# Two neighbouring attentions of a decoder kernel in one block, interleaved by batch slots

## The chip, the cores and the metric

The kernel runs on one core of one Trainium2 chip, in one launch. The metric is device microseconds of the whole launch, the median of several runs; lower is better.

## The reference, cut to what matters

The model is a decoder of four layers with three sublayers each (attention, cross attention, feed forward). Each sublayer takes the rows `x` (16 batches of 128 tokens, width 256), normalises them, and adds its result to `x`. The change is in the first two sublayers:

```python
def _L0_attn_ref(x, Wq, Wk, Wv, Wp, bp):          # "l0a", 16 heads of 16, one chunk of 128 tokens
    phi_q = elu(heads(x @ Wq.T)) + 1.0
    phi_k = elu(heads(x @ Wk.T)) + 1.0
    A = where(tril, einsum('bhncd,bhnsd->bhncs', phi_q, phi_k), 0.0)
    num, den = einsum('bhncs,bhnse->bhnce', A, vh), A.sum(-1) + EPS
    return merge(num / den[..., None]) @ Wp.T + bp

def _L0_xattn_ref(q, k, v, attention_mask, ...):  # "l0x": q from x, k and v from the context
    scores = einsum('bnlh,bnph->bnlp', qm, km) / sqrt(16)
    scores = where(mask, scores, -1e8)
    return merge(einsum('bnlp,bnph->bnlh', softmax(scores), vm)) @ Wo.T + bo
```

Both read the layer norm of `x`: each batch is normalised by the mean and the variance of its own rows, so batch b of l0x needs only batch b of l0a's result.

## The kernel before, in words

All rows stay in one tile `x` on the chip (128 partitions, 256 columns for each of the 16 batches), with a mean and a variance for each batch in `mean_var` (`G.mv`). The program is a chain of stages, listed in `STAGES`. Each stage opens a block in which every engine gets its own instruction list, written out in order; semaphores tie the lists together. At its end `Region.close` (line 82) ends the block, clears the stage's semaphores and puts a barrier over all engines (line 89), so that nothing of a stage runs beside the one before.

Stage l0a is `transposed_attention` (line 263), stage l0x is `softmax_attention` (line 625). Both are software pipelines over the 16 batches, and the engines' lists are loops over a step i. In l0a TensorE does at step i: `scores(i)` (L407), `weigh_values(i-1)` (L427), `transpose_x(i+2)` (L373), `project_out(i-2)` (L436), `project_qk(i+2)` (L389) and `project_v(i+2)` (L395). ScalarE copies the second half of the scores (L500), takes the denominators (L509), the transposed rows (L471) and the exponentials of q and k (L484), and normalises rows for later (L464). VectorE forms the features (L564), masks half of the scores (L576), divides (L580, L583), adds the result to x (L590) and takes its statistics three steps behind (L594, L598). GpSimd spreads the heads (L339), masks the other half (L348) and adds the output bias (L353).

In l0x TensorE does at step i: `scores(i)` (mask L769, products L778), the four `transpose_p(i-1)` (L789) with `weigh_values(i-2)` (L806), `transpose_x(i+2)` (L731) and the projections of batch i+2 (L747, L753, L759) between them, and `project_out(i-2)` (L813). The scores of a batch fill all four banks of `psS`, so `scores(i)` waits for the exponentials of batch i-1. VectorE takes maxima (L1002) and ScalarE the exponentials with their sums (L883), VectorE inverts the sums (L1009), GpSimd scales (L706). Before its loop l0x prepares on VectorE: two normalised batches (L933), the mask as float (L965) and as filling values (L976).

The layer norm needs a square root on ScalarE and an inverse on VectorE. l0a takes them for the first 12 batches in its own tail (`early_roots` L159, `early_inverse` L165); l0x takes the last four at its start (L170, L176). ScalarE loads another function table when it goes from exponentials to roots or back.

PSUM has eight banks. Each of the two stages uses all eight: four for the scores and one each for four other uses.

Of the kernel before, what the change touches and what calls it, by code (L numbers as in the profile page):

```python
# [17 lines left out]
P = 128  # L18
NB = 16
# [133 lines left out]
HEAD = 12  # L153

# [108 lines left out]
def transposed_attention(nc, G, A, tag, kind, w, cross=False, out_bias=False):  # L263
# [6 lines left out]
    if G.next == "l0x":  # L270
        load_early(nc, G, "l0x", attention_loads(nc, G, A, "l0x"))
        loads = loads + G.ahead
# [22 lines left out]
    psS, psXV, psQK, psO, psY = R.ps("psS", [P, 2048]), R.ps("psXV", [P, 512]), R.ps("psQK", [P, 512]), R.ps("psO", [P, 512]), R.ps("psY", [P, 512])  # L295
# [9 lines left out]
    block = R.block()  # L305
# [7 lines left out]
    @block.sync  # L313
    def _(sp):
        for dst, src, sem in loads:
            sp.dma_start(dst, src).then_inc(sem, 16)
        sp.wait_ge(loaded, NL)
        sp.wait_ge(G.context_loaded, 16)

    @block.gpsimd  # L320
    def _(pool):
# [7 lines left out]
        nc.gpsimd.memset(G.pad[:, 0:1], 0.0).then_inc(set_up, 1)  # L329
        pool.wait_ge(loaded, NL)  # L330
# [33 lines left out]
    @block.tensor  # L364
    def _(pe):
# [74 lines left out]
        for i in range(-2, NB + 2):  # L440
            if 0 <= i < NB:
                scores(i)
# [10 lines left out]
    @block.scalar  # L453
    def _(act):
# [59 lines left out]
        for i in range(-2, NB + 1):  # L514
            if not relu2 and 0 <= i < NB:
# [14 lines left out]
        early_roots(nc, G, act, mv_ready, head_ready)  # L530

    @block.vector
    def _(dve):
# [66 lines left out]
        for i in range(-3, NB + 3):  # L600
            if not relu2 and 0 <= i + 1 < NB:
# [13 lines left out]
            if i == NB + 1:  # L615
# [3 lines left out]
        dve.wait_ge(inverse_ready, 1)  # L619
        dve.wait_ge(mv_ready, NB)  # L620

    close_stage(G, R)


def softmax_attention(nc, G, A, tag, kind, w, normed="layer", cross=False, biased=False, out_bias=False, saved=None, ahead=()):
# [12 lines left out]
    st6 = R.sb("st6", [P, 6 * NB])  # L638
    mask2 = R.sb("mask2", [P, 2])
# [7 lines left out]
    rstd, std = G.rstd, G.std  # L647
# [13 lines left out]
    psS, psT, psXV, psQK, psOY = R.ps("psS", [P, 2048]), R.ps("psT", [P, 512]), R.ps("psXV", [P, 512]), R.ps("psQK", [P, 512]), R.ps("psOY", [P, 512])  # L661
# [3845 lines left out]
```

## Time and profile before

| | |
|---|---|
| median of 3 runs | 2493.9 us (2491.03 to 2498.77) |
| profiled execution, span from first to last instruction | 2493.0 us (the profile gives its span alone) |
| TensorE busy over the span | 2221.8 us, 89% |
| VectorE, ScalarE, GpSimd busy | 1680.9, 1318.5, 805.3 us |
| mean granted TensorE clock | 0.944 of full speed |
| stage l0a | from 13.0 to 139.5 us |
| stage l0x | from 140.7 to 310.4 us |

Busy shares are averages over stages with different limits. A timeline line gives a start, a duration, the engine and source line, what is written from what, and in brackets the idle time of the engine before it with what ended it. Where several equal instructions follow each other they stand as one line with a count, and the duration is that of all together.

### The profile page before, as it was taken

What the parts mean: (1) busy time and instruction counts of PE and PEld (TensorE: products, weight loads), DVE (VectorE), ACT (ScalarE), POOL (GpSimd) and SP (SyncE); (2) the same over time, 40 slices, a digit from 0 to 9 for tenths busy, and PEclk for the clock granted to TensorE, in tenths of its full rate; (3) what the DMA queues carried; (4) which work ended last, traced back from release to release, by engine and by line L of the source; (5) the groups of instructions that cost most, each with busy time, mean ns of one, the idle gap of its engine ahead of it and who ended that gap; (6) DMA issues with size and microseconds to landing.
All of it is one profiled execution on the core that took longest, in us unless ns stands there. A gap on an engine that the chain in (4) does not pass through costs nothing. (4 is left out here: it accounts for less than half of the span.)

```text
span 2493.0 us, 48623 instructions
## 1 busy us (share of the span) xinstructions
PE 2221.8 (89%) x17358; PEld 1814.4 (73%) x17360; DVE 1680.9 (67%) x3260; ACT 1318.5 (53%) x3083; POOL 805.3 (32%) x1019
## 2 busy tenths in 40 slices
PE   6979799999699797989999979999779897999875
PEld 5857587887476696778888658888567686788652
DVE  4767544774666586765677646666677785888858
ACT  4558635665477663542666443333476574445335
POOL 4656402333255442100233202222211100544365
PEclk9989879999899898979999999999889999999888
DMA  3000082113400000032211430000200002877711
GB/s 113 2 1 2 1 338 83 52 52 131 147 2 2 22 2 1 2 157 115 100 52 51 163 130 1 2 1 1 102 1 1 1 1 88 229 207 214 230 29 34
DMA packets 102933, 178.37 MB, mean 72 GB/s; under 512 B 59687, under 2 KB 71591, under 8 KB 97578
## 3 DMA queue, kind: packets, MB, share of 16 engines
q1 hardware_dynamic: 85514, 135.93, 16.4%
q0 software_dynamic: 9792, 28.85, 3.6%
q10 hardware_dynamic: 7392, 10.49, 1.2%
q8 instruction: 144, 2.36, 0.4%
q14 instruction: 91, 0.75, 0.1%
HBM read 112.44 MB, written 62.78 MB: 70 GB/s over the span
## 5 line engine op out<-in xcount | busy, mean ns | idle before, releaser
L2356 POOL TENSOR_TENSOR l2a_Pn<-l2a_Pn,l2a_rden 128x1024 f32<-128x1024 f32 x32 | 60.0, 1897 | 288.9 <-DVE l2a_rden L2595 288.9
L1630 ACT ACTIVATE l0f_w_parts<-l0f_W 128x512 fp32r (+1 forms) x117 | 90.4, 775 | 64.8 <-PE l0f_psG L1435 50.4
L1788 DVE TENSOR_TENSOR l0f_w_parts<-l0f_W,l0f_w_parts 128x512 fp32r<-128x512 f32 (+1 forms) x117 | 99.2, 867 | 37.7 <-ACT l0f_w_parts L1630 37.5
L1630 ACT ACTIVATE l1f_w_parts<-l1f_W 128x512 fp32r (+1 forms) x117 | 90.5, 774 | 63.1 <-PE l1f_psG L1435 50.3
L4188 POOL TENSOR_TENSOR l3x_Pn<-l3x_Pn,l3x_fac 128x616 f32<-128x616 f32 (+2 forms) x96 | 70.3, 761 | 150.3 <-DVE l3x_fac L4267 140.6
L1788 DVE TENSOR_TENSOR l1f_w_parts<-l1f_W,l1f_w_parts 128x512 fp32r<-128x512 f32 (+1 forms) x117 | 99.2, 867 | 12.6 <-ACT l1f_w_parts L1630 12.2
L1488 PE MATMUL l1f_psY<-l1f_W,l1f_XT_hT 128*128 (+1 forms) x440 | 104.2, 380 | 0.8 <-ACT l1f_XT_hT L1610 0.8
L883 ACT ACTIVATE l1a_att_Pn<-l1a_att_psS,l1a_att_nmx 128x128 f32<-128x128 f32 x256 | 91.8, 418 | 1.7 <-DVE l1a_att_nmx L1002 1.7
L883 ACT ACTIVATE l0x_Pn<-l0x_psS,l0x_nmx 128x128 f32<-128x128 f32 x256 | 91.7, 418 | 0.9 <-DVE l0x_nmx L1002 0.9
L706 POOL TENSOR_TENSOR l1a_att_Pn<-l1a_att_Pn,l1a_att_rden 128x512 f32<-128x512 f32 x64 | 66.5, 1039 | 72.1 <-DVE l1a_att_rden L1009 72.1
L1488 PEld LDWEIGHTS l1f_psY<-l1f_W,l1f_XT_hT 128*128 128x128 f32 x440 | 80.3, 190 | 10.8 <-issue 1.0
L706 POOL TENSOR_TENSOR l0x_Pn<-l0x_Pn,l0x_rden 128x512 f32<-128x512 f32 x64 | 66.5, 1039 | 51.3 <-DVE l0x_rden L1009 49.3
L1765 DVE TENSOR_TENSOR l1f_work<-l1f_work,l1f_psU 128x512 f32<-128x512 f32 x55 | 37.8, 687 | 64.3 <-PE l1f_psU L1435 41.7
L1368 POOL DMA_INDIRECT results_by_token<-l0f_rows_in_out,l0f_dest x39 | 38.8, 995 | 130.0 <-DVE l0f_rows_in_out L1776 130.0
L1368 POOL DMA_INDIRECT results_by_token<-l1f_rows_in_out,l1f_dest x39 | 38.5, 987 | 130.6 <-DVE l1f_rows_in_out L1776 130.6
L4259 DVE TENSOR_TENSOR_SCAN l3x_cum<-l3x_segments_begin,l3x_Pn 128x1024 f32<-128x1024 f32 x32 | 73.4, 2292 | 8.3 <-ACT l3x_Pn L4119 8.3
L1488 PE MATMUL l0f_psY<-l0f_W,l0f_XT_hT 128*128 x312 | 73.9, 380 | 0.8 <-ACT l0f_XT_hT L1610 0.8
L1359 POOL DMA_INDIRECT l1f_rows_in_out<-rows_by_token,l1f_source x39 | 37.9, 972 | 101.2 <-DVE pad L1853 74.0
L883 ACT ACTIVATION_READ_ACCUMULATOR l0x_Pn<-l0x_psS,l0x_nmx 128x1 f32 x256 | 66.4, 259 | 0.0
L883 ACT ACTIVATION_READ_ACCUMULATOR l1a_att_Pn<-l1a_att_psS,l1a_att_nmx 128x1 f32 x256 | 66.3, 259 | 0.0
L2516 ACT ACTIVATE l2a_Pn<-l2a_Pn 128x1024 f32<-128x1024 f32 x32 | 33.9, 1058 | 59.9 <-DVE l2a_Pn L2587 59.9
L1359 POOL DMA_INDIRECT l0f_rows_in_out<-rows_by_token,l0f_source x39 | 38.1, 977 | 84.8 <-DMA keys<-l0f_rows_in_out 67.5
(883 smaller groups left out, 7652.5 us busy)
## 6 DMA issues: line engine op xcount, KB each, us to landing
relative_rows<-l3x_ext SPq DMA_DIRECT2D x32, 516.0 KB, 5.9
l1f_W<-in_l1f_w SPq DMA_DIRECT2D x9, 1536.0 KB, 20.1
l0f_W<-in_l0f_w SPq DMA_DIRECT2D x8, 1536.0 KB, 26.4
cumulative_rows<-l3x_cum SPq DMA_DIRECT2D x32, 384.0 KB, 3.4
l3x_K<-keys SPq DMA_DIRECT2D x16, 512.0 KB, 5.2
l3x_rel<-relative_rows SPq DMA_DIRECT2D x32, 231.0 KB
values<-l1f_W SPq DMA_DIRECT2D x11, 512.0 KB, 5.6
l3x_V<-values SPq DMA_DIRECT2D x16, 308.0 KB
```

Source lines behind the costliest of these rows:

```text
L706: nc.gpsimd.tensor_tensor(part, part, rden[b % 2][:, 4 * r:4 * r + 4].unsqueeze(2).to_broadcast([P, 4, P]), ALU.mult)\
L883: ins = nc.scalar.activation(Pn[b % 2][:, pos * P:(pos + 1) * P], psS[:, pos * P:(pos + 1) * P], ACT.Exp, bias=nmx[b % 2][:, pos:pos + 1], ...
L1359: nc.gpsimd.indirect_dma_start(X[k % NX][:, :], None, G.XN[:, :], bass.IndirectOffsetOnAxis(source[:, k:k + 1], 0))\
L1368: nc.gpsimd.indirect_dma_start(G.YT[:, :], bass.IndirectOffsetOnAxis(dest[:, k:k + 1], 0), Y[k % NY][:, :], None)\
L1488: ins = nc.tensor.matmul(psY[:, 0:D], hT[n % 2][:, j * P:(j + 1) * P], weights(n, 2 * DC * F + j * D, D), start=(j == 0), stop=(j == FC - 1))
L1630: nc.scalar.activation(w_high[i], W[:, bass.ds(act_offsets[k] + o, m)], ACT.Copy).then_inc(high_ready, 1)
L1765: nc.vector.tensor_tensor(h[n % 2], sg[n % 2], psU[:, :], ALU.mult).then_inc(h_ready, 1)
L1788: nc.vector.tensor_tensor(w_low[i], W[:, bass.ds(dve_offsets[k] + o, m)], w_high[i], ALU.subtract).then_inc(low_ready, 1)
L2356: nc.gpsimd.tensor_tensor(part, part, rden[b % 2][:, 8 * u:8 * u + 8].unsqueeze(2).to_broadcast([P, 8, P]), ALU.mult)\
L2516: nc.scalar.activation(part, part, ACT.Exp, scale=W ** -0.5).then_inc(e_ready, 1)
L4188: nc.gpsimd.tensor_tensor(v, v, fac[n % 3][:, s * HH:(s + 1) * HH].unsqueeze(2).to_broadcast([P, HH, SEG[s]]), ALU.mult)\
L4259: nc.vector.tensor_tensor_scan(cum[i][:, :], segments_begin[:, :], Pn[n % NP][:, :], 0.0, ALU.mult, ALU.add).then_inc(sums_ready, 1)
```

## The change: both stages in one block

The two functions no longer open a block: each returns a `Part` with one generator for each engine, which yields a slot number ahead of each step's instructions. `run_parts` opens one block, and `by_slots` writes each engine's list by drawing from the generators in order of slot, the first attention first at equal slots. The second attention's slots lie 16 (its predecessor's number of batches) behind: its step i is slot 16+i. So on each engine the second's fill (steps -2 and -1) comes in slots 14 and 15, behind the first's own steps there, and its first scores in slot 16. What comes ahead of the first yield (GpSimd's clearing of five value tiles, VectorE's head scales) is written at the start of the block. VectorE prepares the mask in slots 6, 8 and 10. The layer norm's roots for the second attention are taken in two parts: batches 0 to 7 in slot 12 (ScalarE) and 13 (VectorE, with the first two normalised batches), batches 8 to 15 in slots 19 and 20. The first attention's `early_roots` and `early_inverse` go. The PSUM banks are allocated once and used by both; where the second first writes a bank, TensorE waits for the last read of it by the first. The end and the start of a block between the two go, with semaphore clearing and barrier. The first attention of layer 1 and the cross attention of layer 1 use the same functions, each as the single part of its block.

```diff
+FIRST = 8
+
+def by_slots(*programs):
+    todo = [[next(program) + offset, k, program, offset] for k, (program, offset) in enumerate(programs)]
+    while todo:
+        now = min(todo, key=lambda entry: entry[:2])
+        slot = next(now[2], None)
+        if slot is None:
+            todo.remove(now)
+        else:
+            now[0] = slot + now[3]
+
+def run_parts(nc, G, *parts):
+    offsets = [0]
+    for part in parts[:-1]:
+        offsets.append(offsets[-1] + part.slots)
+    K = Region(nc, "parts")
+    block = K.block()
...
+    @block.tensor
+    def _(pe):
+        by_slots(*[(part.tensor(pe), o) for part, o in zip(parts, offsets)])
...
+def attention_banks(R):
+    return {name: R.ps(name, [P, size]) for name, size in (("psS", 2048), ("psXV", 512), ("psQK", 512), ("psM", 512), ("psN", 512))}
...
 def transposed_attention
+    def projections_read(eng):
+        eng.wait_ge(xnT_ready, NB)
+        eng.wait_ge(v_ready, NB)
+    def queries_read(eng):
+        eng.wait_ge(qk_ready if relu2 else qk_taken, NB)
+    def scores_read(eng):
+        eng.wait_ge(pa_raw if relu2 else pa_ready, NB)
+        eng.wait_ge(pb_raw, NB)
+    def sums_read(eng):
+        eng.wait_ge(oT_ready, NB)
+        eng.wait_ge(den_ready, NB)
+    def rows_read(eng):
+        eng.wait_ge(x_ready, NB)
...
         for i in range(-2, NB + 1):
+            yield i
...
-        early_roots(nc, G, act, mv_ready, head_ready)
+        if last:
+            early_roots(nc, G, act, mv_ready, head_ready)
...
 def softmax_attention: tensor
             if b >= 1:
                 pe.wait_ge(v_ready, b)
+            elif before:
+                before.projections_read(pe)
...
         def scores(b):
+            if b == 0 and before:
+                before.scores_read(pe)
...
 scalar
-        if layer:
+        if before:
+            yield -4
+            act.wait_ge(before.moments_ready, FIRST)
+            nc.scalar.activation(std[:, 0:FIRST], variances(G)[:, 0:FIRST], ACT.Sqrt, bias=G.neg1e5[:, 0:1]).then_inc(first_roots, 1)
+        elif layer:
             late_roots(nc, G, std_ready)
...
             new, now, mid = i + 2 < NB, 0 <= i < NB, 0 <= i - 1 < NB
+            yield i
+            if before and i == 3:
+                act.wait_ge(before.moments_ready, NB)
+                nc.scalar.activation(std[:, FIRST:], variances(G)[:, FIRST:], ACT.Sqrt, bias=G.neg1e5[:, 0:1]).then_inc(std_ready, 1)
...
 vector
-        normalise(0)
-        normalise(1)
-        if layer:
-            late_inverse(nc, G, dve, step, std_ready)
+        if before:
             head_scales()
+            yield -10
+        else:
+            normalise(0)
+            normalise(1)
+            if layer:
+                late_inverse(nc, G, dve, step, std_ready)
+                head_scales()
...
             step.do(nc.vector.memset(ones[:, :], 1.0))
+            yield -8
...
+            yield -6
             step.do(nc.vector.tensor_scalar(fill[:, :], mbc[:, :], -1.0, piece[:, 0:1], ALU.add, ALU.mult))
...
+            yield i
+            if before and i == -3:
+                dve.wait_ge(first_roots, 1)
+                nc.vector.reciprocal(rstd[:, 0:FIRST], std[:, 0:FIRST]).then_inc(first_inverse, 1)
+                dve.wait_ge(first_inverse, 1)
+                dve.wait_ge(before.moments_ready, FIRST)
+                normalise(0)
+                normalise(1)
+            if before and i == 4:
+                dve.wait_ge(before.moments_ready, NB)
+                dve.wait_ge(std_ready, 1)
+                step.do(nc.vector.reciprocal(rstd[:, FIRST:], std[:, FIRST:]))
...
+def first_attentions(nc, G, A):
+    C = Region(nc, "l0")
+    banks = attention_banks(C)
+    G.held.append(C)
+    load_early(nc, G, "l0x", attention_loads(nc, G, A, "l0x"))
+    parts = [transposed_attention(nc, G, A, "l0a", "linear", "l0a_", out_bias=True, banks=banks, last=False)]
+    parts.append(softmax_attention(nc, G, A, "l0x", "masked", "l0x_", cross=True, biased=True, out_bias=True, banks=banks, before=parts[0]))
+    run_parts(nc, G, *parts)
...
-    "l0a": lambda nc, G, A: transposed_attention(nc, G, A, "l0a", "linear", "l0a_", out_bias=True),
-    "l0x": lambda nc, G, A: softmax_attention(nc, G, A, "l0x", "masked", "l0x_", cross=True, biased=True, out_bias=True),
+    "l0a": first_attentions,
+    "l0x": lambda nc, G, A: None,
```

## Rows read from the trace of the kernel before

**Rows 1.** Stages: us, busy by engine (count), PEclk, DMA share, GB/s.

```profile
13.00:140.70 127.70, 114.26 (x1696) 94.72 (x1696) 78.36 (x117) 62.73 (x117) 70.00 (x73) 0.98 0.07 26
...
140.70:311.60 170.90, 145.99 (x1504) 112.94 (x1504) 115.97 (x300) 123.04 (x596) 99.64 (x117) 0.93 0.01 2
```

**Rows 2.** Timeline, end of the first attention: start us, us, engine, line, op.

```profile
131.13 0.30 PE L427 MATMUL l0a_psO<-l0a_PTa,l0a_V 128*32 128x128 f32 x2 [1.86 <-DVE l0a_oT L583]
...
136.11 0.17 DVE L598 BATCH_NORM_AGGREGATE mean_var<-l0a_st 128x2 f32<-128x6 f32 x1
...
136.22 0.43 DVE L594 BATCH_NORM_STATS2 l0a_st<-x 128x6 f32<-128x256 f32 x1
...
139.36 0.18 DVE L598 BATCH_NORM_AGGREGATE mean_var<-l0a_st 128x2 f32<-128x6 f32 x1
```

**Rows 3.** Timeline, start of the second attention.

```profile
140.73 1.74 POOL L688 MEMSET l0x_V<- 128x512 f32 x3 [11.05 <-POOLq L89]
...
140.77 1.24 DVE L933 TENSOR_SCALAR l0x_xn<-x,mean_var,rstd 128x256 f32<-128x256 f32 x2 [1.23 <-PEq L89]
...
142.52 1.51 DVE L965 CAST l0x_mbc<-l0x_w_m 128x2048 f32<-128x2048 uint8 x1
...
145.07 1.29 DVE L976 TENSOR_SCALAR l0x_fill<-l0x_mbc,l0x_piece 128x2048 bf16<-128x2048 f32 x1
...
148.14 0.41 PE L731 MATMUL l0x_psXV<-ident,l0x_xn 128*128 128x128 f32 x2 [0.69 <-DVE l0x_V L996]
...
151.88 0.40 PE L769 MATMUL l0x_psS<-l0x_fill,l0x_ones 32*128 32x512 bf16 x4
```

**Rows 4.** Timeline, TensorE at batches 14 and 15 of the first attention.

```profile
120.30 1.15 PE L407 MATMUL l0a_psS<-l0a_bd,l0a_qk 32*128 32x256 f32 x16
...
121.37 0.30 PE L427 MATMUL l0a_psO<-l0a_PTa,l0a_V 128*32 128x128 f32 x2
...
124.32 1.15 PE L407 MATMUL l0a_psS<-l0a_bd,l0a_qk 32*128 32x256 f32 x16
```

**Rows 5.** Timeline, first softmax batch up to the second's scores.

```profile
153.21 1.29 DVE L1002 TENSOR_REDUCE l0x_nmx<-l0x_psS 128x4 f32<-128x512 f32 x2 [0.29 <-PE l0x_psS L778]
...
155.77 1.19 PE L747 MATMUL l0x_psQK<-l0x_xnT,l0x_w_Wq 128*128 128x128 f32 x8 [2.26 <-ACT l0x_xnT L863]
...
156.76 1.90 PE L753 MATMUL l0x_psQK<-ctxT,l0x_w_Wk 128*128 128x128 f32 x8
...
158.46 1.88 PE L759 MATMUL l0x_psXV<-l0x_w_Wv,ctxT 128*128 128x256 f32 x4
...
160.28 0.39 PE L769 MATMUL l0x_psS<-l0x_fill,l0x_ones 32*128 32x512 bf16 x4
```

**Rows 6.** Timeline, ScalarE and VectorE waits in a first-attention batch.

```profile
114.66 1.02 ACT L500 ACTIVATE l0a_PTb<-l0a_psS 128x1024 f32<-128x1024 f32 x1 [0.61 <-PE l0a_psS L407]
...
119.54 0.60 ACT L484 ACTIVATE l0a_ex<-l0a_psQK 128x512 f32<-128x512 f32 x1 [2.24 <-PE l0a_psQK L389]
...
120.65 0.69 DVE L564 SCALAR_TENSOR_TENSOR l0a_qk<-l0a_ex,l0a_re 128x512 f32<-128x512 f32 x1 [0.97 <-ACT l0a_re L485]
```

**Rows 7.** Timeline, ScalarE: table loads and root at the boundary.

```profile
133.64 1.28 ACT L159 ACT_TABLE_LOAD   x1
...
134.93 0.30 ACT L159 ACTIVATE std<-mean_var,ln_eps 128x12 f32<-128x12 f32 x1
...
151.76 1.28 ACT L883 ACT_TABLE_LOAD   x1
```

**Rows 8.** Timeline, ScalarE between two softmax batches.

```profile
177.72 0.74 ACT L872 ACTIVATE l0x_qk<-l0x_psQK,l0x_w_bq 128x128 f32<-128x128 f32 x2
...
180.01 0.60 ACT L891 ACTIVATE l0x_PT<-l0x_psT 128x512 f32<-128x512 f32 x1 [1.55 <-PE l0x_psT L789]
...
180.50 0.36 ACT L883 ACTIVATE l0x_Pn<-l0x_psS,l0x_nmx 128x128 f32<-128x128 f32 x1
```

**Rows 9.** A stretch of low granted clock, columns of Rows 1.

```profile
156.00:160.00 4.00, 4.00 (x20) 3.47 (x19) 1.80 (x5) 4.00 (x25) 2.84 (x3) 0.60 0.00 0
```

More of the change, by code:

```diff
@@ L304, in transposed_attention @@
     s_step, p_step = R.sem("dve_step"), R.sem("pool_step")
-    block = R.block()
+    part = Part(R, loads, loaded, NL)
+    part.slots, part.moments_ready = NB, mv_ready
+    def projections_read(eng):
[11 more added lines that the diff above has]
+        eng.wait_ge(x_ready, NB)
+    part.projections_read, part.queries_read, part.scores_read, part.sums_read, part.rows_read = projections_read, queries_read, scores_read, sums_read, rows_read
     NV = 4
@@ L311, in heads, with gpsimd @@
         return 4 * r + 2 * c
[L313 to L321, printed above, removed]
+    def gpsimd(pool):
         step = Step(pool, p_step)
@@ L362, in _, with tensor @@
                 add_bias(i)
-    @block.tensor
-    def _(pe):
+    def tensor(pe):
+        yield -2
         pe.wait_ge(loaded, NL)
@@ L614, in _ @@
                 add_y(i - 2)
-            if i == NB + 1:
+            if last and i == NB + 1:
                 early_inverse(nc, G, dve, head_ready, inverse_ready)
@@ L618, in _, with softmax_attention @@
                 moments(i - 3)
-        dve.wait_ge(inverse_ready, 1)
+        if last:
+            dve.wait_ge(inverse_ready, 1)
         dve.wait_ge(mv_ready, NB)
-    close_stage(G, R)
-def softmax_attention(nc, G, A, tag, kind, w, normed="layer", cross=False, biased=False, out_bias=False, saved=None, ahead=()):
+    part.gpsimd, part.tensor, part.scalar, part.vector = gpsimd, tensor, scalar, vector
+    return part
+def softmax_attention(nc, G, A, tag, kind, w, normed="layer", cross=False, biased=False, out_bias=False, saved=None, ahead=(), banks=None, before=None):
     masked = kind == "masked"
@@ L670, in softmax_attention @@
     s_step, p_step = R.sem("dve_step"), R.sem("pool_step")
-    block = R.block()
+    part = Part(R, loads, loaded, NL)
+    part.slots, part.moments_ready = NB, mv_ready
     scale = HD ** -0.5
@@ L676, in heads, with gpsimd @@
         return 4 * r + 2 * c
-    @block.sync
-    def _(sp):
-        for dst, src, sem in loads:
-            sp.dma_start(dst, src).then_inc(sem, 16)
-        sp.wait_ge(loaded, NL)
-    @block.gpsimd
-    def _(pool):
+    def gpsimd(pool):
         step = Step(pool, p_step)
@@ L721, in _, with tensor @@
                 add_bias(i)
-    @block.tensor
-    def _(pe):
+    def tensor(pe):
+        yield -2
         pe.wait_ge(loaded, NL)
@@ L800, in weigh_values @@
                 pe.wait_ge(x_ready, b)
+            elif before:
+                before.rows_read(pe)
             for c in range(DC):
```

74 lines of the change are left out of this document (56 added, 18 removed).

## The prediction

> **What bounds the kernel now.** I read the page first: its busy shares are averages over the whole program, and the chain of waits covers only the last 80 us, so neither says what this change is worth. The stage table does [rows 1]. While the first attention runs, TensorE is busy for 114 of 128 us at nearly full clock; in the second for 146 of 171 us, with ScalarE at 123. The reader is to see that TensorE's idle time in the first stage is 13.4 us and that it lies at the two ends. The timeline of the boundary shows where [rows 2]: the last batch is weighed at 131.13, after TensorE waited 1.86 us for the division, and the stage's last moment is finished at 139.54. Then barrier and fill [rows 3]: GpSimd starts at 140.73, VectorE makes the mask (1.51 us, then 1.29 us), the second batch's fill starts on TensorE at 148.14, and the first softmax scores only at 151.88.
>
> **The time between two marks.** One mark is the start of scores of batch 14 in the first attention, at 120.30 [rows 4]; the other the start of the second scores of the softmax attention, at 160.28 [rows 5]. Before it is 39.98 us. I build the same stretch from the new lists of TensorE.
>
> Slot 14: scores, weighing and output projection as now, 124.32 - 120.30 = 4.02 us [rows 4]. Behind them the fill of softmax batch 0. Its price is the fill of batch 1 at full clock, 151.88 - 148.14 = 3.74 us [rows 3]. Together 7.76. What the fill waits for on the banks (last rows, values and projections of batch 15 copied) is done in slot 13, so I take that wait as nothing; at worst it is the copy and its handshake, 0.6 us. Slot 15 is the same: 7.76. In slot 16 weighing and projection come first, 124.32 - 121.37 = 2.95 us [rows 4]. So the softmax scores start at 120.30 + 18.47 = 138.77, against 151.88: 13.11 us earlier. This takes with it the barrier, the mask, the late normalising and the division waits, since TensorE has other work during each.
>
> **Maxima come late in slot 16.** VectorE finishes the first attention's step ahead of them. Batch 15 is weighed from 135.82 on; from there to the end of add and moment it is 136.28 - 131.13 = 5.15 us [rows 2], so the first maxima start at 140.97. By the old distance from scores to maxima, 153.21 - 151.88 = 1.33 us [rows 3, 5], they would start at 140.10. Loss: 0.87 us. From maxima to the second scores nothing changes, as TensorE waits for the exponentials there: 8.40 us from scores to scores, so the second mark would be at 138.77 + 0.87 + 8.40 = 148.04.
>
> **What is left of the first attention in slots 17 and 18.** Statistics 0.43 and moment 0.17 us [rows 2], and an add, taken as long as the statistics, stand ahead of the maxima of slot 17, and 0.60 of the same ahead of those of slot 18. All on the path would be 1.63 us, all hidden 0. ScalarE takes a transposed block before it needs the maxima (0.5 us, from 180.01 to 180.50 [rows 8]), which hides about that much each time: 0.6 and 0.2, so 0.8 us.
>
> **Preparations moved into the first attention.** In a steady step VectorE idles 0.97 us before the features [rows 6]. In slot 6 the mask conversion (1.51 [rows 3]) and two smaller instructions, for which I take 0.5, push the features by about 1.0; in slot 10 the filling values (1.29) by 0.3; the three small ones of slot 8 fit in. Behind the features stand the masking of scores, and on GpSimd the spreading; TensorE needs both a step later, so TensorE's order hides it: 0, at most 1.1 us for each. GpSimd's clearing of five tiles (three take 1.74 us [rows 3]) stands at the block's start, where it has nothing to spread yet. The roots in slot 12: load 1.28 and root 0.30 [rows 7] follow the copy of values, where ScalarE idles 0.61 us [rows 6], so the copy of scores comes 0.95 late; the masking by GpSimd behind it is needed a step later. Exponentials come back in slot 13, where ScalarE idles 2.24 us [rows 6]: hidden. VectorE's inverse (some 0.2) and two normalised batches (1.24 [rows 3]) in slot 13 stand against the 0.97 idle, 0.5 late, hidden likewise. Sum 0; with the cover gone it is the 0.95 plus 0.5. SyncE issues the same loads in the same order, and its waits hold nothing else.
>
> **The second half of the roots, slot 19.** This sits in the softmax loop, where ScalarE is on the path. Now: q taken until 178.46, the transposed block from 180.01, exponentials from 180.50 [rows 8]. After: a load of 1.28 and the root of 0.30 fill the idle 1.55; the block goes at 180.04; a load of 1.28 before the exponentials puts them at 181.92: 1.42 us late, and every batch after it. Bounds: 0 if TensorE has slack there, 2.86 if nothing is covered. At the old boundary both loads were beside waits.
>
> The trace puts no gap around a load: the one at 151.76 has no idle time before it, and the root at 134.93 starts with the load's end [rows 7].
> The Trainium skill, "ScalarE: Activation LUTs", section "What ACT_TABLE_LOAD costs", adds a drain of about 1.38 us to each load of 1.28. By that the slot would cost 2.76 us more; the trace does not agree so far.
>
> **The clock.** When TensorE had idled 2.26 us before the projections at 155.77, the engine's granted clock fell, to a mean of 0.60 from 156 to 160 [rows 5, 9], the upper level of 2.4 GHz and the lower of 1.2 mixed, and the projections took 1.70 and 1.82 instead of 0.99 (k and v against q). It was hidden then. In the new slot 16 the idle is 3.1 us (2.26 + 0.87), so I expect the same fall. Projections start at 138.77 + 0.87 + 3.89 (155.77 - 151.88) = 143.53; q 0.99, k 1.70, v 1.88, and behind them, newly, the first attention's last output projection, as long as v: 1.88. They end at 149.98, 1.94 us behind the mark of 148.04. At full clock they end near 147.4 and cost nothing. I take 1.94; bounds 0 and 3.0 (all four at the low level).
>
> **Sum.** 13.11 - 0.87 - 0.80 - 0 - 1.42 - 1.94 = 8.08 us. The profiled span is 2493.0; after it 2484.9. The median of the runs is 0.9 above the span, which I take as what lies around it: 2493.9 - 8.1 = 2485.8. Later stages move earlier as a whole; no transfer was started by the clock of a stage before them (GB/s is 2 in the second stage [rows 1]).
>
> **Rivals.**
> - The clock holds in slot 16: 10.0 us gained, 2483.9. For it, work is denser before the idle time than in the old slot; against it, the idle is longer.
> - Each switch of tables holds ScalarE longer in the loop than the 1.28 shown. If as much again per switch (2.56), the gain is 5.5: 2488.4. For it: the loop is the one place where exponentials stand right on both sides; against it rows 7. The Trainium skill's section named above states such an addition.
> - The overlap doesn't do what it says: VectorE, in order, waits for the fill's values and keys of slot 14 and 15 before masking the first attention's scores, and TensorE waits for those; fill and drain alternate. Then only what lies between 139.54 and the start of a fill 3.74 us before 148.14 goes, 4.9 us, of which 1.42 and 0.80 are paid back: 2.7 us, 2491.2. Against it: the values come 1 us before the scores TensorE issues next.
> - Slower: the clock falls in slot 16 or at the switch in slot 19 and stays low. A batch holds 146 / 16 = 9.1 us of TensorE work at 0.93 [rows 1] in a period of about 9 (8.40 for the first [rows 3, 5]), so at the lower level (k took 1.70 against 0.99) it takes some 15.5 us, 6.5 lost. From two such batches on the gain of 10.0 is gone; 13 lost is 2497. Against it: the fall within 156 to 160 [rows 9] was over by the scores at 160.28, whose four mask products took 0.39 us as those at 151.88 took 0.40 [rows 3, 5].
>
> **How the numbers follow.** Chances: forecast 0.42, clock holds 0.26, longer switch 0.13, alternating 0.11, slower 0.08. What a measurement can tell from no change is 0.3%, 7.5 us: faster means under 2486.4. The forecast lies 0.6 us beyond it, and the runs of before spread over 7.7 us, so I give its case 0.6 faster, the clock case 0.85, the switch 0.2, and the others none beyond noise: 0.25 + 0.22 + 0.03 and a little, 0.52 faster. Slower by over 7.5 us needs three low batches: 0.07. The rest, 0.41, is within. The range: below, the clock case with slots 17 to 19 half hidden (another 1.1) and the spread of a median, 2480.5; above, the alternating case with some of that spread, 2492.0.
>
> **What would show it.** In the profile after: softmax scores near 138.8 and second scores near 149 to 150; no idle time on TensorE over 1 us from 120 to 139 but for the transposes; loads in slots 12, 13 and two in slot 19, with the distance between score starts there 1.4 longer than beside it; first maxima behind the moment of batch 13. Wrong would be: TensorE waiting in slots 14 or 15 for VectorE, steps of slots 6 to 13 longer than before, or a low granted clock beyond slot 17.

## The result and the profile after

In the first comparison the changed kernel took 2485.28 us (median of 8 runs, 2481.32 to 2489.73) against 2493.72 (8 runs, 2487.62 to 2498.77): ratio 0.9967, 95% interval 0.9954 to 0.998, which is 5.0 to 11.5 us faster. The forecast was 2485.8. A later comparison on another chip gave 2481.52 (5 runs, 2478.22 to 2482.98) against 2492.31 (11 runs): 0.9949, interval 0.9936 to 0.9961. The profiled execution spans 2483.9 us, 9.1 less than before.

The stage windows of the changed kernel, cut where the first softmax scores start and where the last ends; the columns are those of [rows 1]:

```profile
13.00:138.80 125.80, 118.68 (x1737) 99.38 (x1738) 81.54 (x128) 65.92 (x124) 74.48 (x82) 1.00 0.07 25
138.80:300.90 162.10, 137.07 (x1465) 105.90 (x1464) 111.90 (x290) 122.57 (x591) 93.57 (x109) 0.96 0.01 2
```

The first attention's stretch now holds 41 more matmul records (the two fills) in 1.9 us less, and TensorE idles 7.1 us in it instead of 13.4 [rows 1]. Its mean granted clock is 1.00 instead of 0.98.

TensorE's timeline of the changed kernel shows the two fills and the first slot with both attentions. To be compared with [rows 3 to 5]:

```profile
120.59 1.15 PE L484 MATMUL l_psS<-l0a_bd,l0a_qk 32*128 32x256 f32 x16
...
125.37 1.16 PE L834 MATMUL l_psQK<-l0x_xnT,l0x_w_Wq 128*128 128x128 f32 x8 [0.47 <-ACT l0x_xnT L961]
...
128.22 1.15 PE L484 MATMUL l_psS<-l0a_bd,l0a_qk 32*128 32x256 f32 x16
...
138.80 0.39 PE L858 MATMUL l_psS<-l0x_fill,l0x_ones 32*128 32x512 bf16 x4
...
143.45 1.69 PE L834 MATMUL l_psQK<-l0x_xnT,l0x_w_Wq 128*128 128x128 f32 x8 [3.02 <-ACT l0x_xnT L961]
144.93 1.92 PE L840 MATMUL l_psQK<-ctxT,l0x_w_Wk 128*128 128x128 f32 x8
146.64 1.37 PE L846 MATMUL l_psXV<-l0x_w_Wv,ctxT 128*128 128x256 f32 x4
147.84 1.03 PE L513 MATMUL l_psN<-l0a_w_Wo,l0a_oT 128*128 128x256 f32 x4
148.80 0.39 PE L858 MATMUL l_psS<-l0x_fill,l0x_ones 32*128 32x512 bf16 x4
```

Slots 14 and 15 take 7.63 us each (128.22 - 120.59), the fill standing behind the first attention's own step without any wait but the 0.47 for the transposed rows. The softmax scores start at 138.80 and the second ones at 148.80. In between TensorE idles 3.02 us, and of the four groups of products behind the idle time the first ones are slow: q takes 1.69 us instead of 1.16, k 1.92 instead of 1.06, the values 1.37 instead of 1.03. The projection at 147.84 is at full speed again (1.03).

What became of each interval, from score starts of both timelines. Only the starts of scores are in the table; slots are those of the changed kernel:

| stretch | before | after | saved |
|---|---|---|---|
| scores of batch 14 to first softmax scores | 120.30 to 151.88 = 31.58 | 120.59 to 138.80 = 18.21 | 13.37 |
| slot 16 | 8.40 | 10.00 | -1.60 |
| slots 17 and 18 | 17.85 | 17.97 | -0.12 |
| slot 19 (two table loads) | 8.99 | 10.42 | -1.43 |
| slot 20 | 9.00 | 9.12 | -0.12 |
| slot 21 to the last softmax scores | 90.96 | 90.96 | 0 |
| sum | | | 10.10 |

So the change is worth 10.1 us up to the last softmax scores (277.27 against 287.08, and 0.29 that the changed kernel was late at its batch 14, where the table begins). From the last softmax scores to TensorE's first product in stage l0f it is 24.30 us against 25.22, another 0.9 gained. From there to its first product in l3f this execution took 1.7 us more than the one before (2104.44 against 2102.73). Experiments 3 and 10 show that two executions of one program can differ by more than that, so it can't be put down to the change. With these pieces the 9.1 us between the spans are accounted for to 0.1.

VectorE in slot 16, and at the start of slot 17:

```profile
138.38 1.75 DVE L659 RECIPROCAL l0a_rden<-l0a_den 128x256 f32<-128x256 f32 x1 [1.15 <-ACT l0a_den L587]
...
140.83 0.17 DVE L677 BATCH_NORM_AGGREGATE mean_var<-l0a_st 128x2 f32<-128x6 f32 x1
140.93 1.25 DVE L1109 TENSOR_REDUCE l0x_nmx<-l_psS 128x4 f32<-128x512 f32 x2
...
149.62 0.17 DVE L677 BATCH_NORM_AGGREGATE mean_var<-l0a_st 128x2 f32<-128x6 f32 x1
150.13 1.29 DVE L1109 TENSOR_REDUCE l0x_nmx<-l_psS 128x4 f32<-128x512 f32 x2 [0.35 <-PE l_psS L867]
```

The maxima of slot 16 start right behind the first attention's moment, 2.13 us behind the scores instead of 1.33: 0.80 late. In slot 17 the leftovers are over before the scores are there: VectorE waits 0.35 us for TensorE.

ScalarE with its table loads, in slot 12 and in slot 19:

```profile
114.36 1.28 ACT L945 ACT_TABLE_LOAD   x1
115.66 0.30 ACT L945 ACTIVATE l0x_std<-mean_var,ln_eps 128x8 f32<-128x8 f32 x1
115.86 1.01 ACT L578 ACTIVATE l0a_PTb<-l_psS 128x1024 f32<-128x1024 f32 x1
...
167.13 1.28 ACT L996 ACT_TABLE_LOAD   x1
168.43 0.30 ACT L996 ACTIVATE l0x_std<-mean_var,ln_eps 128x8 f32<-128x8 f32 x1
168.66 0.60 ACT L989 ACTIVATE l0x_PT<-l_psM 128x512 f32<-128x512 f32 x1
169.27 1.28 ACT L981 ACT_TABLE_LOAD   x1
170.56 0.37 ACT L981 ACTIVATE l0x_Pn<-l_psS,l0x_nmx 128x128 f32<-128x128 f32 x1
```

Loads and their neighbours follow each other within 0.02 us. That is the place of the forecast's 1.42 us.

Two windows of the changed kernel show the low granted clock in slot 16, and the full one in slot 19 behind 1.96 us of idle time, with TensorE's queries there:

```profile
144.00:148.00 4.00, 4.00 (x19) 3.83 (x18) 1.57 (x4) 4.00 (x23) 2.53 (x3) 0.59 0.00 0
172.00:176.00 4.00, 3.59 (x26) 3.17 (x27) 3.16 (x9) 4.00 (x22) 2.37 (x3) 1.00 0.00 0
```

```profile
172.40 1.16 PE L834 MATMUL l_psQK<-l0x_xnT,l0x_w_Wq 128*128 128x128 f32 x8 [1.96 <-ACT l0x_xnT L961]
```

### The profile page after: what moved, and what is told of

The parts are those of the page before. It is cut to its first block and busy times, and to the rows that moved or that the text cites. A ratio compares the mean times of both kernels' runs of the same rounds, so it can differ in the third digit from the quotient of the medians.

```text
span 2483.9 us, 48616 instructions
## 1 busy us (share of the span) xinstructions
PE 2216.7 (89%) x17358; PEld 1810.0 (73%) x17360; DVE 1678.0 (68%) x3260; ACT 1322.2 (53%) x3085; POOL 803.3 (32%) x1019
## 3 DMA queue, kind: packets, MB, share of 16 engines
q8 instruction: 144, 2.36, 0.4%
## 5 line engine op out<-in xcount | busy, mean ns | idle before, releaser
L981 ACT ACTIVATE l0x_Pn<-l_psS,l0x_nmx 128x128 f32<-128x128 f32 x256 | 91.7, 417 | 3.3 <-DVE l0x_nmx L1109 3.3
L1608 PEld LDWEIGHTS l1f_psY<-l1f_W,l1f_XT_hT 128*128 128x128 f32 x440 | 80.3, 190 | 10.8 <-issue 1.0
L981 ACT ACTIVATION_READ_ACCUMULATOR l0x_Pn<-l_psS,l0x_nmx 128x1 f32 x256 | 66.1, 258 | 0.0
```

The costliest lines, as they stand in the source:

```text
L981: ins = nc.scalar.activation(Pn[b % 2][:, pos * P:(pos + 1) * P], psS[:, pos * P:(pos + 1) * P], ACT.Exp, bias=nmx[b % 2][:, pos:pos + 1], ...
L1608: ins = nc.tensor.matmul(psY[:, 0:D], hT[n % 2][:, j * P:(j + 1) * P], weights(n, 2 * DC * F + j * D, D), start=(j == 0), stop=(j == FC - 1))
```

## The experiments

Kernels 1 to 8 were each executed once with a profile, beside one execution of the kernel before on the same chip (2496.45 or 2496.2 us). A total from one execution says little, as the runs of one kernel spread over 5 to 11 us, so their verdicts rest on distances within the first 280 us, taken from the scores of batch 14. These distances repeat: in a second profile of the changed kernel on another chip (kernel 9) the one to the last softmax scores is 156.88 us instead of 156.68.

### 1. The second attention three slots later

Its fill and first scores then have none of the first attention's work beside them; the block, the prepared mask and the two-part roots stay.

```diff
-        offsets.append(offsets[-1] + part.slots)
+        offsets.append(offsets[-1] + part.slots + 3)
...
```

The lines left out move the yields of roots and mask by as many slots the other way, so these stay where they were.

> One block as in the changed kernel, but the second attention's steps lie 19 slots behind instead of 16, with its mask and first roots left in slots 6 to 12. TensorE then fills only behind the first attention's last projection. Theory: barrier and preparations are one part of what was gained, the fill beside the drain's waits the larger one. Drain as in the kernel before, to about 138.4 us, then two fills of 3.7 to 6.6 us by the clock: first softmax scores at 146 to 149 instead of 138.8, span 2484 + 8 = 2492 or so. Rival: what was gained is the block's end and the preparations, and the interleaving is worth little: first scores within 2 us of 138.8 and span at 2484 to 2486.

Measured: 2498.12 us beside 2496.45. TensorE around the first softmax scores, and in the slot with the table loads:

```profile
148.07 0.39 PE L858 MATMUL l_psS<-l0x_fill,l0x_ones 32*128 32x512 bf16 x4
...
180.04 2.08 PE L834 MATMUL l_psQK<-l0x_xnT,l0x_w_Wq 128*128 128x128 f32 x8 [1.97 <-ACT l0x_xnT L961]
```

The batch-14 scores of this execution are 1.10 us later than before's, so the softmax scores come 4.9 us earlier than before (151.88 - 148.07 + 1.10). That is what the missing barrier and the moved preparations bring by themselves. The other 8.5 of the 13.4 us comes with the interleaving. It includes what the clock gives: from 136 to 144 us the granted clock is 0.88 and 0.70 here, where the change has 1.00 and 0.99. Without the interleaving next to nothing remains: the slot with the table loads costs 11.82 us here instead of 8.99, and at the last softmax scores 1.5 us of the 4.9 is left (121.40 to 286.66 is 165.26 us, before it is 166.78). About half of what that slot loses is the table swap (1.43 in the change); the other 1.4 is a fall of the clock, 0.58 from 180 to 184 us, which the change does not have there.

### 2. One slot earlier

```diff
-        offsets.append(offsets[-1] + part.slots)
+        offsets.append(offsets[-1] + part.slots + -1)
...
```

Here too the lines left out keep roots and mask in their slots.

> The second attention's steps lie 15 slots behind instead of 16, its mask and first roots stay in slots 6 to 12. Theory: TensorE's only long idle stretch left (3.0 us at 140.4) comes from exponentials that start late, so an earlier first softmax batch fills it with the first attention's last weighing and projection: first scores near 136.8, second near 146 instead of 148.8, span 2 to 3 us less, 2481 to 2482. Rival: PSUM handover and in-order VectorE bring new waits (scores of batch 0 behind the last masked scores, transposes behind the last division), which eat it: second scores at 148 or later, span 2484 or more.

Measured: 2486.88 us. TensorE:

```profile
137.33 0.39 PE L858 MATMUL l_psS<-l0x_fill,l0x_ones 32*128 32x512 bf16 x4
...
141.98 2.08 PE L834 MATMUL l_psQK<-l0x_xnT,l0x_w_Wq 128*128 128x128 f32 x8 [3.03 <-ACT l0x_xnT L961]
...
149.28 0.39 PE L858 MATMUL l_psS<-l0x_fill,l0x_ones 32*128 32x512 bf16 x4
```

Taken from the scores of batch 13 (114.35 here, 113.74 in the change), the first softmax scores come 2.08 us earlier, the second 0.13 earlier and the last 1.05 later: the first attention's last batch now stands, with weighing and division, inside the first softmax batch, and TensorE runs out of work there just the same. The forecast of 2 to 3 us less was wrong: the second scores are not earlier by more than 0.13 us, as the rival had it. Sixteen slots is the best distance of the three.

### 3 and 10. The mask prepared late

VectorE's cast and filling values in slot 13, against the first attention's work, instead of slots 6, 8 and 10.

```diff
-            yield -10
+            yield -3
...
-            yield -8
+            yield -3
...
-            yield -6
+            yield -3
```

> Undoes one part: VectorE prepares the whole mask (some 3.9 us) in slot 13, ahead of the roots' inverse and the first two normalised batches, instead of in slots 6, 8 and 10. Theory: in slots 6 to 10 it costs nothing because TensorE needs VectorE's results a step later, while 3.9 us at once run past that slack of about 2 to 3 us: the scores of batch 15 or the weighing of batch 14 start 1 to 2 us late, span 2485 to 2486. Rival A: hidden here too, second scores at 148.8 within 0.2. Rival B: no slack at all, 3.9 us late, span 2488.

Measured: 2479.13 us. VectorE, with the features behind all of it:

```profile
120.07 1.19 DVE L1070 CAST l0x_mbc<-l0x_w_m 128x2048 f32<-128x2048 uint8 x1
...
122.29 1.29 DVE L1083 TENSOR_SCALAR l0x_fill<-l0x_mbc,l0x_piece 128x2048 bf16<-128x2048 f32 x1
...
124.51 0.68 DVE L643 SCALAR_TENSOR_TENSOR l0a_qk<-l0a_ex,l0a_re 128x512 f32<-128x512 f32 x1
```

The features come at 124.51 instead of about 121, and TensorE's next scores still start 7.63 us behind the last ones (120.76 to 128.39); to the last softmax scores it is 156.77 us against 156.68. Even this heavier load in one slot is hidden, where 1 to 2 us of delay had been expected (rival A was right). The 6.5 us that the total lies below the change's are made where the edit touches nothing: from TensorE's first product in l0f to its first in l3f this execution took 2097.50 us, the change's 2104.44. So I ran the same kernel again, timed:

> The mask preparations moved to slot 13 once more, now timed in five rounds. Its one profiled execution was 6.5 us below the change's, all of it in stages that the edit doesn't touch. Theory (that was the later stages' wander): median within 2 us of the change's on this chip, about 2485. Rival (each program keeps its own time in the later stages, because its code lies otherwise or its stages start at another phase of the clock): it stays 4 us or more below the change, and the later stages' marks agree with those of the single execution to under 1 us.

Measured: 2484.04 us (6 runs, 2478.9 to 2485.68), 2.5 above the change on the same chip (within 2 had been expected), with widely overlapping runs. Its profiled execution took 2105.87 us from l0f to l3f: the same program, on another chip, 8.4 us apart in the same stages. On the one chip its six runs already spread over 6.8 us. That excludes the rival that each program keeps its own time in the later stages: the later stages wander from execution to execution, and no difference of a few us in them may be put down to an edit of the first attentions.

### 4. The root from the logarithm

The inverse root as exp(-0.5 ln(v)), for one table if both functions shared it with the exponentials.

```diff
-            nc.scalar.activation(std[:, 0:FIRST], variances(G)[:, 0:FIRST], ACT.Sqrt, bias=G.neg1e5[:, 0:1]).then_inc(first_roots, 1)
+            nc.scalar.activation(std[:, 0:FIRST], variances(G)[:, 0:FIRST], ACT.Ln, bias=G.neg1e5[:, 0:1]).then_inc(first_roots, 1)
+            act.wait_ge(first_roots, 1)
+            nc.scalar.activation(rstd[:, 0:FIRST], std[:, 0:FIRST], ACT.Exp, scale=-0.5).then_inc(first_inverse, 1)
...
```

The second eight roots are edited in the same way, and VectorE's two inverses go.

> The second attention's inverse roots are taken on ScalarE as exp(-0.5 ln(v + eps)), two functions that one table can hold, instead of root and inverse; everything else is as in the changed kernel. Theory: the 10.42 us between the softmax scores of batches 3 and 4, against 8.99 beside them, is the two table loads of slot 19 less 1.4 us of idle time: the distance becomes 8.99 to 9.1 and everything behind moves 1.4 us, and the 0.13 us of the inverse in slot 20 goes too; span 2482.4. Rival: the 1.43 us is the wait for the first attention's last moments in slot 19, or the compiler loads a table for each of the two functions: the distance stays at 10.4 or grows.

Measured: 2486.72 us. ScalarE:

```profile
114.55 1.28 ACT L945 ACT_TABLE_LOAD   x1
...
116.16 1.28 ACT L947 ACT_TABLE_LOAD   x1
...
170.08 1.28 ACT L998 ACT_TABLE_LOAD   x1
...
171.69 1.28 ACT L1000 ACT_TABLE_LOAD   x1
```

A load stands ahead of the logarithm and another ahead of the exponential behind it, so nothing is saved, as the rival had it: slot 19 takes 10.53 us. It shows the price of bad cover, however. The two loads in slot 12, with only the logarithm between them, lengthen the stretch from the scores of batch 13 to those of batch 14 from 6.85 to 8.20 us, where one load in slot 12 and one in slot 13 had cost nothing.

Slot 16, which the edit does not touch, takes 11.32 us here instead of 10.00:

```profile
144.99 2.08 PE L834 MATMUL l_psQK<-l0x_xnT,l0x_w_Wq 128*128 128x128 f32 x8 [3.04 <-ACT l0x_xnT L963]
```

Behind the same idle time as in the change (3.04 against 3.02 us) k and the values take 1.91 us each and the first attention's projection 1.45; the granted clock is 0.53 from 144 to 148 and 0.61 from 148 to 152, where the change has 0.59 and 1.00. So the same idle time ahead of the same products can cost 1.3 us more in one kernel than in another.

### 5. Roots without ScalarE

A guess from the bits of the variance and three Newton steps on VectorE, spread over slots 11, 12, 19 and 20; no table load is left there.

```diff
-                nc.scalar.activation(std[:, FIRST:], variances(G)[:, FIRST:], ACT.Sqrt, bias=G.neg1e5[:, 0:1]).then_inc(std_ready, 1)
...
+                step.do(nc.vector.tensor_scalar(y.bitcast(U32), v.bitcast(U32), -0.5, 1597463007.0, ALU.mult, ALU.add))
...
+                step.do(nc.vector.tensor_tensor(t, y, y, ALU.mult))
+                step.do(nc.vector.scalar_tensor_tensor(t, t, -0.5, v, ALU.mult, ALU.mult))
+                step.do(nc.vector.scalar_tensor_tensor(y, t, 1.5, y, ALU.add, ALU.mult))
...
```

> The second attention's inverse roots are worked out on VectorE alone, from a guess by the bits of the number and three Newton steps (eleven small instructions for each half), in pieces put ahead of places where VectorE waits anyway; ScalarE has no root and no table load between slots 12 and the end. Theory: the distance between the softmax scores of batches 3 and 4 falls from 10.42 to 9.0 us, that of 4 and 5 from 9.12 to 9.0, everything behind is 1.4 to 1.6 us earlier than in the changed kernel from one mark to the other. Rival: the small instructions are too long for VectorE's waits, the maxima of the next banks go late and half or more of the 1.4 us comes back.

Measured: 2480.99 us. Slot 19 takes 9.09 us instead of 10.42, slot 20 takes 9.65 instead of 9.12. VectorE in slot 20 shows why:

```profile
176.82 1.25 DVE L1122 TENSOR_REDUCE l0x_nmx<-l_psS 128x4 f32<-128x512 f32 x2
177.99 0.35 DVE L1021 TENSOR_TENSOR l0x_tmp<-l0x_rstd 128x8 f32<-128x8 f32 x1
178.38 0.54 DVE L1022 SCALAR_TENSOR_TENSOR l0x_tmp<-l0x_tmp,l0x_std 128x8 f32<-128x8 f32 x1
178.95 0.54 DVE L1023 SCALAR_TENSOR_TENSOR l0x_rstd<-l0x_tmp,l0x_rstd 128x8 f32<-128x8 f32 x1
179.52 0.69 DVE L1135 COPY l0x_PT<-l_psM 128x512 f32<-128x512 f32 x1
```

The three small operations stand ahead of the copy that TensorE's weighing waits for. Two of them take 0.54 us each. The same three on the same columns take 0.16, 0.17 and 0.17 us in slot 19 (from 170.48 on). GpSimd is at work from 176.58 to 179.46 and idle from 170.35 to 171.33, and each of these small operations in this trace that falls into idle time of GpSimd takes 0.13 to 0.17 us. That points at GpSimd's work beside them as what makes them long; no run sets it apart. The table swap did cost what slot 19 showed: 1.33 of it comes back, and 0.53 is paid in slot 20.

### 6, 7 and 8. The idle time ahead of the second batch's queries

Three ways to deal with TensorE's 3.02 us. Kernel 6 moves the first attention's last output projection into it. Kernel 7 lets VectorE take the first maxima ahead of add and moment, so that the idle time gets shorter. Kernel 8 fills it with six products whose result nobody reads.

```diff
+++ 6
-                yield i
+                yield i - 0.5 if not last and i == NB + 1 else i
...
+                if before and i == 0:
+                    yield 0.5
+++ 7
+                divide_o(i - 1)
+                if not last and i == NB:
+                    yield i + 0.5
...
+++ 8
+                if before and i == 0:
+                    pe.wait_ge(qk_ready, 2)
+                    for k in range(6):
+                        nc.tensor.matmul(psQK[:, 0:D], G.ctxT[:, 0:P], wv[:, 0:D], start=True, stop=True)
```

> The first attention's last output projection stands on TensorE in slot 16 ahead of the second's query projection, where TensorE idles 3.0 us, instead of at the start of slot 17. Theory: of the 1.60 us that the first softmax batch takes longer than the 8.40 of before, 0.80 are the late maxima and 0.80 this projection behind half-clock projections; the second scores come 0.8 us earlier, at 148.0 (by marks counted from the first attention's scores at 120.59), even if the clock falls again. Rival: the second scores wait for the exponentials alone and all 1.60 us are the late maxima: 148.8 as before.

> VectorE takes the first two maxima of the softmax ahead of the first attention's product, add and moment of slot 16 (1.0 us), the division stays ahead of them. Theory: maxima at 140.1 instead of 140.93, exponentials 0.8 us earlier; if the clock still falls, the projections run from 142.65 and the second scores come 0.8 us earlier, 148.0. Rival: the path of slot 16 is the half-clock projections alone, which fall at a fixed time: the second scores stay at 148.8.

> Adds work whose result nobody reads: six products of 128x256 (0.48 us each, 2.9 in all) on TensorE in slot 16, in the 3.0 us of idle time ahead of the query projection. Theory: the granted clock falls because of that idle time; filled, it stays at 1.00 from 144 to 148, the projections there take 0.9, 0.9 and 1.0 us instead of 1.5, 1.7 and 1.2, and the second scores come 0.8 us earlier, at 148.0. Rival: the clock falls on its own schedule or by the load, or the added work delays the projections: clock near 0.6 again or second scores at 148.8 or later.

Measured: 2482.91, 2487.91 and 2483.36 us. TensorE of kernel 6, then two of its windows:

```profile
141.32 1.10 PE L513 MATMUL l_psN<-l0a_w_Wo,l0a_oT 128*128 128x256 f32 x4 [0.64 <-DVE x L669]
143.70 1.16 PE L834 MATMUL l_psQK<-l0x_xnT,l0x_w_Wq 128*128 128x128 f32 x8 [1.28 <-ACT l0x_xnT L963]
...
147.89 0.38 PE L858 MATMUL l_psS<-l0x_fill,l0x_ones 32*128 32x512 bf16 x1 [0.94 <-ACT l0x_Pn L983]
```

```profile
144.00:148.00 4.00, 3.06 (x27) 2.38 (x27) 2.16 (x6) 4.00 (x24) 2.78 (x3) 1.00 0.00 0
172.00:176.00 4.00, 4.00 (x22) 3.97 (x22) 2.29 (x7) 3.81 (x21) 2.72 (x3) 0.61 0.00 0
```

With one piece of work between two shorter waits the clock holds at 1.00 from 144 to 148, and what is late next is ScalarE's exponentials (0.94 us). Kernel 8 holds it as well:

```profile
140.55 2.75 PE L929 MATMUL l_psQK<-l0x_w_Wv,ctxT 128*128 128x256 f32 x12
143.74 1.16 PE L834 MATMUL l_psQK<-l0x_xnT,l0x_w_Wq 128*128 128x128 f32 x8 [0.44 <-ACT l0x_xnT L965]
```

From the first softmax scores to the third it is 18.12 us in the change, 17.12 in kernel 6, 17.14 in kernel 8. So the fall of the clock in slot 16 costs the change 1.0 us of path. That useless work gives the same as moved work shows that the idle time brings the fall and that nothing else of kernel 6 gave the gain.

All of it and more is lost in slot 19: 11.85 us in both kernels (11.86 in kernel 7) against 10.42. The idle time there is 1.96 us in kernel 6 and 1.97 in the others, as in the change (all waited for the table loads), but now the clock falls behind it:

```profile
171.64 2.04 PE L834 MATMUL l_psQK<-l0x_xnT,l0x_w_Wq 128*128 128x128 f32 x8 [1.96 <-ACT l0x_xnT L963]
```

From 172 to 176 the granted clock is 0.61 in kernel 6, where the change had 1.00. This is no accident of one execution. In kernels 3, 9 and 10, whose products in these slots are the change's, it stayed at 1.00 behind 1.96 or 1.97 us and slot 19 took 10.42 or 10.43 us; in kernels 1, 6, 7 and 8 it fell each time. Kernel 7 had its fall in slot 17:

```profile
143.55 1.16 PE L839 MATMUL l_psQK<-l0x_xnT,l0x_w_Wq 128*128 128x128 f32 x8 [2.34 <-ACT l0x_xnT L966]
...
152.10 1.73 PE L839 MATMUL l_psQK<-l0x_xnT,l0x_w_Wq 128*128 128x128 f32 x8 [0.90 <-ACT l0x_xnT L966]
```

After 2.34 us of idle time the queries ran at full clock, and after 0.90 us one slot later they didn't. Its third scores come 17.88 us behind the first: 0.24 gained, and 1.44 lost in slot 19. Together with the kernels above, that says: which idle time the fall follows is not told by its length alone. What tells it, these runs leave open.

### 9, 11 and 12. Both edits together

Kernel 9 is the change itself, kernel 11 joins kernels 5 and 6, kernel 12 joins kernels 5 and 8: no table loads in slot 19 and no long idle time in slot 16. All were timed in five rounds on one chip beside kernel 10 and the kernel before, which took 2492.31.

> The changed kernel itself, timed in five rounds beside the kernel before and the next three on one chip. Theory (the gain is made in the first two attentions and is about 0.33%): some 8 to 10 us below the kernel before on this chip. Rival (the later stages wander by several us from program to program, and a good part of the 8.4 us was such wander): the difference on this chip is under 6 us or over 11 us.

> Two edits together: the first attention's last-but-one output projection goes into TensorE's idle time ahead of the second's first queries (slot 15.5), and the roots are taken on VectorE by Newton steps, so ScalarE loads no other table in slots 12, 13 and 19. Theory (the clock falls after idle time of about 2 us or more, and each edit takes one such place away): from the scores of batch 14 to the last softmax scores 155.0 us (157.10 in the run with the projection alone, less 11.85 - 9.09 in slot 19, plus 0.64 for the pieces), against 156.68 for the change; the median some 1.7 us below the change on this chip, more if the later stages begin well. Granted clock 1.00 in every stretch from 136 to 184 us. Rival (a fall of the clock that is taken away at one place comes at the next idle time, as it did with the projection alone, where slot 19 paid it): a stretch with 0.6 to 0.8 remains, 156.4 us, median within 0.5 us of the change.

> The same with six extra products (a result that nobody reads) in TensorE's idle time ahead of the second's first queries instead of the moved projection, and the Newton roots. Theory: 157.30 of the run with the extra products alone, less 2.76 in slot 19, plus 0.64: 155.2 us from the scores of batch 14 to the last softmax scores, granted clock 1.00 from 136 to 184 us, median within 0.5 us of the previous kernel. Rival (the fall moves on): a stretch at 0.6 to 0.8 remains and the distance is 156.5 or more.

| kernel | median us (runs, lowest to highest) | ratio to before, interval | batch-14 scores to last but one softmax scores | to last |
|---|---|---|---|---|
| 9, the change | 2481.52 (5, 2478.22 to 2482.98) | 0.9949 (0.9936 to 0.9961) | 146.85 | 156.88 |
| 11 | 2480.31 (5, 2476.33 to 2486.36) | 0.9945 (0.9932 to 0.9958) | 145.00 | 153.93 |
| 12 | 2483.01 (6, 2479.88 to 2488.91) | 0.9962 (0.9948 to 0.9976) | 145.02 | 154.87 |

TensorE of kernel 11, and the two windows in which the others fell:

```profile
143.92 1.16 PE L834 MATMUL l_psQK<-l0x_xnT,l0x_w_Wq 128*128 128x128 f32 x8 [1.29 <-ACT l0x_xnT L961]
```

```profile
144.00:148.00 4.00, 3.16 (x23) 2.48 (x23) 2.38 (x6) 4.00 (x25) 3.00 (x3) 1.00 0.00 0
...
172.00:176.00 4.00, 3.89 (x33) 3.05 (x35) 3.24 (x9) 3.71 (x19) 2.35 (x3) 1.00 0.00 2
```

All twelve windows of 4 us from 136 to 184 stand at 1.00 in kernels 11 and 12. With both idle times away the fall doesn't move on to a third place in this stretch. Up to the last but one scores they are 1.85 and 1.83 us shorter than the change; in kernel 11 that is 1.01 from slots 16 and 17, 1.34 from slot 19, less 0.50 in slot 20. The last slot gave kernel 11 another 1.1 us: behind the same idle time as in the change (2.36 and 2.35 us) its transposes took 0.63 instead of 1.09 us and its output projection 1.22 instead of 1.92. That was not planned, so its 153.93 against 155.0 expected is in part luck. In the total nothing of this can be told: 1.2 us below the change and 1.5 above it, in runs that spread by 5 to 10. Kernel 11 is the best in the stretch that was worked on and has the lowest median, but it isn't shown to be faster than the change. Two expectations on totals were missed: the change lay 10.8 us below the kernel before, above the 8 to 10 expected and under the rival's 11, and kernel 12's median lay 2.7 above kernel 11's, where 0.5 was expected; the spread of the runs covers both.

## Why the prediction was right, step by step

The time (2485.28 against 2485.8) and the mechanism were right. Three terms were near (13.11, 0.87 and 1.42), two losses were priced too high (0.80 and 1.94), and one small loss was missing. The traces give 10.1 us for the part that the sum was made for, the forecast 8.08. The median of the first comparison gave 8.4, that of the second 10.8. The closeness of the forecast to the first median is thus in part luck; the intervals of the two comparisons meet at 9.7 to 11.5 us, around the traced value.

- **Slots 14 to 16 up to the first softmax scores, 13.11 us.** Measured 13.37. The slots took 7.63 instead of 7.76, twice; no bank was waited for. Experiment 1 divides it: 4.9 for barrier and preparations, 8.5 with the interleaving.
- **Late maxima, 0.87.** Measured 0.80, at the place named.
- **Leftovers in slots 17 and 18, 0.80.** Measured 0.12. This step failed: I charged whatever ScalarE's own work didn't hide (and 1.03 - 0.5 and 0.6 - 0.5 make 0.63, not 0.8). But VectorE had time ahead of the scores, and only an operation that runs past the scores' end can delay the maxima. In slot 17 they waited 0.35 us for TensorE. In slot 18 they came 2.50 us behind the scores instead of 2.03, and of these 0.47 us only 0.12 reached the path.
- **Moved preparations, 0.** Slots 6 to 13 keep their 6.85 us (113.74 to 120.59), and experiment 3 shows that all of the mask in one slot would be hidden too. Experiment 4 shows where the cover ends: 1.28 + 0.21 us more on ScalarE in slot 12 cost 1.35.
- **The table swap in slot 19, 1.42.** Measured 1.43. Experiment 5, without the loads, gets 1.33 of it back. The rival of a longer switch falls as well, since the loads abut their neighbours. The Trainium skill, "ScalarE: Activation LUTs", section "What ACT_TABLE_LOAD costs", adds a drain of about 1.38 us to each; no run here shows it.
- **The clock in slot 16, 1.94.** It fell as expected, behind 3.02 us of idle time, but came back sooner: q was slow (1.69), which I had left at full clock, the values took 1.37 instead of 1.88, and the last projection 1.03 instead of 1.88. On the mark's distance the loss is 0.80, and by experiments 6 and 8 the fall costs 1.0 over two slots. This term failed by its size: I had taken all three groups behind q to be as slow as the slowest rows of before, though [rows 9] ended with the scores at full clock. Such a price does occur, though: kernel 4's slot 16 took 11.32 us, against 11.21 by the forecast (8.40 + 0.87 + 1.94). What decides between the two the runs leave open.
- **Not in the sum.** VectorE's inverse of the second eight roots stands ahead of the maxima in slot 20, with a wait of 0.21 us behind it:

```profile
178.57 0.17 DVE L1158 RECIPROCAL l0x_rstd<-l0x_std 128x8 f32<-128x8 f32 x1
...
178.95 1.29 DVE L1109 TENSOR_REDUCE l0x_nmx<-l_psS 128x4 f32<-128x512 f32 x2 [0.21 <-DVE l0x_rstd L1158]
```

  The maxima come 1.76 us behind the scores instead of 1.38 one slot later, and slot 20 takes 0.12 us more. It was an instruction in the diff that I had not priced. The inverse alone is not the cost: in kernels 3 and 10 it stands at the same place with a wait of 0.04 us or less behind it, the maxima come 1.59 us behind the scores, and slot 20 takes 9.01 and 8.99 us. Why the wait of 0.21 us is missing there stays open.
- **The rivals.** That the clock holds was wrong for the change, though its 10.0 us are what the traces gave, by another sum. The alternating fill is excluded by the 7.63 us of slots 14 and 15. The slow rival's trigger was real and its price wrong: with the clock fallen in slot 19, as kernels 1, 6, 7 and 8 show, the slot lost 1.4 us more and not 6.5; in kernel 6 the clock was at 1.00 again from 176 to 180.

## What to carry to other kernels

When two pipelines follow each other, look first at laying the second's fill beside the first's drain, not at the barrier between them: here 8.5 us against 4.9, and of the 4.9 only 1.5 were left at the last softmax scores without the interleaving. Then price each engine's list at the joint: an operation of the first that stands ahead of the second's critical one costs at most what runs past that one's own releaser, and here 0.21 us of such delay cost nothing and 0.47 us cost 0.12. A small operation also has no fixed price: the same one took 0.17 us in one slot and 0.54 in the next. And make distances between marks within the stage the measure, when the whole program wanders by more than the edit is worth.

## What the runs showed of the hardware

The granted clock of TensorE fell behind 3.02 to 3.04 us of idle time in slot 16 of the change and of kernel 4. The fall cost the change 1.0 us of path (against kernels 6 and 8); kernel 4, with the same idle time and the same products, lost 1.3 us more. In slot 19 the fall cost 1.4 us. Of two equal idle times of 1.96 us before the same products, one was followed by 1.00 (the change) and one by 0.61 (kernel 6), and both outcomes repeat: 1.00 in kernels 3, 9 and 10 too, a fall in kernels 1, 7 and 8 too. After 2.34 us it stayed at 1.00 in kernel 7. Products that nobody reads, laid in the idle time, held it at 1.00.

Small VectorE operations of 128x8 took 0.13 to 0.17 us while GpSimd stood idle and up to 0.54 us while it worked (kernel 5).

One program in two executions, on two chips, took 2097.5 and 2105.9 us over the same later stages. Its cause stays open.
